# Placing q's high parts from ScalarE's queue in a sliding-window attention kernel

## What is computed

```python
x = L0_attn_hidden_states
xn = _layernorm(x, axis=-1)
# attention
q = _interleaved_rope(q, cos, sin) * SCALE
k = _interleaved_rope(k, cos, sin) * SCALE
scores = jnp.einsum('bquh,bkuh->buqk', q, k)
sw_mask = jnp.abs(pos[:, None] - pos[None, :]) <= SW
scores = jnp.where(sw_mask[None, None, :, :], scores, NEG)
combined = jnp.concatenate([scores, sink_logits], axis=-1)
probs = jax.nn.softmax(combined.astype(jnp.float32), axis=-1)
out = jnp.einsum('buqk,bkuh->bquh', attn, v)
s = jnp.einsum('bquh,uhm->bqm', out, Wo) + bo
# gate
g = _silu(_L0_ffn_ref(xn, L0_ffn_weight, L0_ffn_weight_scale, L0_ffn_bias))
x = x + s * g
```

## Time and profile before

| | us |
|---|---|
| median of three runs | 2087.06 |
| lowest and highest of them | 2068.41, 2089.49 |
| the profiled execution, device time | 2074.46 |
| its span, first to last instruction | 2072.7 |
| TensorE busy, of the span | 1807.7 (87%) |
| VectorE busy | 1277.2 (62%) |
| GpSimd busy | 1011.2 (49%) |
| ScalarE busy | 730.8 (35%) |
| mean granted TensorE clock | 0.907 of full speed |

### The profile page before, as it was taken

One profiled execution on the slowest core, in us unless ns is written; L12 is line 12 of the kernel. 1 busy time (PEld: TensorE's weight loads), 2 busy tenths in 40 slices (PEclk: granted clock), 3 DMA queues, 4 the chain that ended last, 5 costly groups with the idle time before them and its releaser, 6 DMA issues.

```text
span 2072.7 us, 34158 instructions
## 1 busy us (share of the span) xinstructions
PE 1807.7 (87%) x11139; PEld 1592.2 (77%) x11139; DVE 1277.2 (62%) x4157; ACT 730.8 (35%) x1509; POOL 1011.2 (49%) x1019
## 2 busy tenths in 40 slices
PE   2498999989899889898889989898999988899888
PEld 1287878877788777787778878887788877788777
DVE  7755665655656557556566665665666666565564
ACT  2133333333333433333333333343343333333332
POOL 3345444554444644545544553554455465445441
PEclk8579899989998899889999999998999999999899
DMA  4634334344254343443344343344335434442530
GB/s 145 129 68 69 65 63 83 72 78 74 37 94 70 67 78 51 81 75 67 68 78 80 57 88 65 59 92 84 60 53 95 80 64 71 77 66 54 95 65 17
DMA packets 81728, 151.95 MB, mean 73 GB/s; under 512 B 13712, under 2 KB 30864, under 8 KB 77456
## 3 DMA queue, kind: packets, MB, share of 16 engines
q1 hardware_dynamic: 81552, 149.76, 39.8%
HBM read 18.64 MB, written 4.19 MB: 11 GB/s over the span
## 4 chain that ended last, share of the span: by engine, by line
PE 68%; issue 6%; DVE 6%; SPq 5%; ACT 4%; DMA 4%; POOL 3%; POOLq 0%; DVEq 0%
PE pv_bank L1132 23%; PE ring L1093 10%; PE acc L1155 8%; PE ring L1044 8%; PE score L1116 7%; PE score L1118 6%; PE ring L1142 3%; SPq L364 3%; ACT stage L619 2%; PE ring L1053 2%; DMA qT_full<-q_second_hi 2%; DMA kT_low<-k_second 2%; POOL k_first L520 1%; POOL k_second L522 1%; SPq L366 1%
## 5 line engine op out<-in xcount | busy, mean ns | idle before, releaser
L854 DVE CUSTOM_DVE_ANT_0 junk<-ring,mask 128x384 bf16<-128x384 f32 (+1 forms) x1024 | 497.3, 488 | 646.1 <-PE ring L1093 636.2
L1132 PEld LDWEIGHTS pv_bank<-v,stage 128*128 128x128 f32 x5120 | 708.3, 206 | 14.4 <-issue 5.8
L1132 PE MATMUL pv_bank<-v,stage 128*128 128x65 f32 x5120 | 713.8, 282 | 0.6 <-DVE o_norm L886 0.4
L542 POOL TENSOR_SCALAR_AFFINE_SELECT stage<-stage 128x512 f32<-128x512 f32 x384 | 246.8, 656 | 833.9 <-ACT stage L619 833.7
L1093 PE MATMUL ring<-kT_high,qT_full 128*128 128x384 f32 (+1 forms) x1024 | 411.6, 403 | 165.9 <-DMA kT_low<-k_second 71.0
L619 ACT ACTIVATE stage<-score 128x512 f32<-128x512 f32 x640 | 357.5, 597 | 335.5 <-PE score L1118 334.0
L1093 PEld LDWEIGHTS ring<-kT_high,qT_full 128*128 128x128 f32 x1024 | 213.2, 208 | 209.0 <-issue 129.7
L1116 PE MATMUL score<-qT_full,kT_high 128*128 128x512 f32 x640 | 279.0, 436 | 16.1 <-ACT stage L619 14.1
L660 ACT ACTIVATE oT_hi<-ring 128x256 fp32r<-128x256 f32 x256 | 98.6, 385 | 518.5 <-PE ring L1142 518.5
L1118 PE MATMUL score<-qT_high,kT_low 72*128 72x512 f32 x640 | 267.8, 418 | 0.0
L1116 PEld LDWEIGHTS score<-qT_full,kT_high 128*128 128x128 f32 x640 | 132.2, 207 | 68.9 <-ACT stage L619 48.7
(11 more groups left out here) (119 smaller groups left out, 2651.9 us busy)
## 6 DMA issues: line engine op xcount, KB each, us to landing
qT_high<-qT_full SPq DMA_DIRECT2D x64, 512.0 KB, 4.5
qT_full<-q_first SPq DMA_DIRECT2D x64, 256.0 KB, 4.2
qT_full<-q_first_hi SPq DMA_DIRECT2D x64, 256.0 KB, 5.6
qT_full<-q_second SPq DMA_DIRECT2D x64, 256.0 KB, 6.9
qT_full<-q_second_hi SPq DMA_DIRECT2D x64, 256.0 KB, 8.0
kT_high<-k_first_hi SPq DMA_DIRECT2D x128, 64.0 KB, 3.3
kT_high<-k_second_hi SPq DMA_DIRECT2D x128, 64.0 KB, 3.1
qT_high<-turned_rows SPq DMA_DIRECT2D x512, 2.0 KB
```

Source lines behind the costliest of these rows:

```text
L542: nc.gpsimd.affine_select(out=pr, in_=pr, compare_op=ALU.is_ge, fill=0.0, base=0, pattern=[[0, GROUP], [sign, P]], channel_multiplier=-sign) \
L854: nc.vector.tensor_tensor_reduce(junk[:, h % 2, 0:cols], ring[h % 2][:, 0:cols], mask[:, m0:m0 + cols], 1.0, LOWEST, ALU.add, ALU.max, row ...
L1132: last = nc.tensor.matmul(pv[:, h, :], prob[:, q % 2 * 3 + n, h * P:(h + 1) * P], v[:, slot, k, :], start=(n == 0), stop=(n == len(BLOCKS[ ...
```

## The change

SyncE's `queries_in` becomes `lows_in`, which issues only the two transfers of low parts. ScalarE gets `highs_placed(a)`, which issues the two transfers of high parts on its own queue, with the same waits on the scores and on the earlier transfers, and with `s_first_hi` and `s_second_hi` (its own roundings) where SyncE waited for the low parts. It stands in quarter 3 of ScalarE's program, behind `o_high` and ahead of `keys_high`. Sizes, tiles, semaphores and counts of transfers are the same.

```diff
-            def queries_in(a):
+            def lows_in(a):
-                parts = ((0, q_first, q_first_hi, s_first_lo, s_qT_first_in),
-                         (HALF, q_second, q_second_hi, s_second_lo, s_qT_second_in))
                 upto(sp, s_score_pe, NB * (a - 1))
-                for row, low, high, ready, done in parts:
+                for row, low, ready, done in ((0, q_first, s_first_lo, s_qT_first_in),
+                                              (HALF, q_second, s_second_lo, s_qT_second_in)):
                     sp.wait_ge(ready, a + 1)
                     upto(sp, done, Q_IN * a)
                     sp.dma_start(qT_full[row:row + HALF, a % 2, :, :].bitcast(F32), low[:, :]).then_inc(done, 16)
-                    sp.dma_start(qT_full[D + row:D + row + HALF, a % 2, :, :].bitcast(F32), high[:, :]) \
-                        .then_inc(done, 16)
...
+            def highs_placed(a):
+                upto(act, s_score_pe, NB * (a - 1))
+                for row, high, ready, done in ((D, q_first_hi, s_first_hi, s_qT_first_in),
+                                               (D + HALF, q_second_hi, s_second_hi, s_qT_second_in)):
+                    act.wait_ge(ready, a + 1)
+                    upto(act, done, Q_IN * a)
+                    nc.scalar.dma_start(qT_full[row:row + HALF, a % 2, :, :].bitcast(F32), high[:, :]) \
+                        .then_inc(done, 16)
...
                     if q == 1 and real(a):
                         first_high(a)
                         second_high(a)
+                    if q == 3 and real(a):
+                        highs_placed(a)
                     if q == 3 and k in (2, 6) and quad < BATCH * QUADS:
                         keys_high(quad)
```

More of the change, by code:

```diff
@@ L415, in step @@
                 if real(a):
-                    queries_in(a)
+                    lows_in(a)
                 if real(t) and t % QUAD == 0:
```

## The result

The changed kernel takes 2124.69 us (median; 2120.65 to 2142.23), the kernel before 2087.28 us beside it. The ratio is 1.0217, 95% interval 1.0147 to 1.0288: slower by about 45 us, 31 to 60. On a second chip, beside 25 executions of the kernel before, it was 1.0254 (1.0173 to 1.0334). The profiled execution has a span of 2120.1 us against 2072.7, 47.4 more, at a mean clock of 0.908 against 0.907.

The account below looks back on a forecast made before the run. It took TensorE to be bound by its stalls, chiefly waiting for q's landing and the keys, and by its clock. Terms summing to 64.8 us were added to the profiled 2074.46, giving 2139, rounded to 2140; range 2080 to 2190.

Parts of the forecast that it names:

- q's landing is what the first row product waits for: TensorE's unnamed wait is the landing of q's last high part; SyncE's two fewer issues, 1.3 us a step, gain 0.
- k = 3 and 4: 16 boundaries: highs queue behind the lows on the DMA engines, the four need the same 9.96 us, change 0.
- k = 5, 7, 0 and 1: Highs issued behind `o_high` land later at these boundaries, delaying the first row product: 9.6, 6.3, 2.1 and 2.4 us.
- ScalarE held for 1.3 us by two issues: At k = 2 and 6 `keys_high` queues behind the issues, moving 15 boundaries by 1.3 us: 19.5 us.
- ScalarE's next instruction starts at once behind the issues: Sign in the profile after, on ScalarE's queue, that would show the forecast wrong; no size given.
- The rival that the issue is free: Issuing on ScalarE costs nothing and the clock holds; only landings count, 20.4 us, 2095 us; chance 0.24.
- `x_in` ahead of the highs: At k = 7 the load of `x_in` is issued before the highs and competes with them: 1 us, six boundaries, 6 us.
- The clock, 18.9 us: New stalls at k = 5 and 7 drop half of TensorE's full-clock steps there to the low clock: 18.9 us.
- The rival of two queues that add up: Two DMA queues carry more than one, so q's highs land sooner and stalls go: about 2009 us; chance 0.07.
- stalls of 1.1: Sign in the profile after: the first row product at k = 7 and 0 stalls 1.1 us each.

Follow-up runs that it names:

- the repeat: The changed kernel timed once more, unaltered, beside the kernel before on the second chip: 2135.34 us, ratio 1.0254.

## Why the prediction was right, and where its terms were off

It said 2140 us, slower, with 64.8 us added; measured were 37.4 us between the medians, about 45 by the ratio, and 51 between the means on the second chip. Direction and the main mechanism hold; the sum was too large, and that the time came within 16 us of the forecast is in part luck: the sum was added to the fast profiled execution, and on the median of the three runs it would have given 2152. Term by term (the 61 boundaries read here lack one of the eight that it counted at k = 5, and have one more at k = 0 and at k = 1):

- *q's landing is what the first row product waits for; nothing is gained from SyncE's lighter queue.* Right. It is shown by the highs issued with the lows: two issues less on SyncE, and a first row product at 10.06 instead of 10.01. The window that it cites for busy DMA engines (1132 to 1138) lies behind a step with k = 0, not k = 3; behind the one with k = 3 (1223 to 1229) it is the same, share 1.07 and 133 GB/s.
- *k = 3 and 4: no change, since the highs queue behind the lows' bytes.* Right, 10.01 and 10.02.
- *k = 5, 7, 0 and 1: landings 1.2, 0.9, 0.3 and 1.2 us late, 20.4 us.* The mechanism is right, the size about three times too large: the late start on one queue added 6.8 us of stalls at these k. Two inputs of the one formula failed. The issue was put 0.06 us behind the *end* of `o_high`, 0.45 behind its start; it leaves 0.08 behind its start, 0.37 sooner. And the first row product comes 5.96 us behind the first issue, not 6.12 (k = 5: 1310.11 - 1304.15). Together 0.53 off each of the four numbers: for k = 5 that gives 0.68, and it moved by 0.69; for k = 0 it gives less than nothing. With one queue and the same late start, k = 7 moved by 0.2 and k = 0 not at all.
- *ScalarE held for 1.3 us by two issues, 19.5 us at k = 2 and 6.* Held for 1.07, since the first issue overlaps `o_high`; stalls grew by 18.8. That the number fits is part luck: 15 times 1.07 is 16, and the rest arises further down the chain, where at k = 6 GpSimd's subtraction ends 1.5 us later (8.25 against 6.76 behind q's first issue, medians) though the rounding starts 1.07 later. Why is open. Swapping the order of the two showed it as the cause: 19 us of stalls gone at k = 2 and 6 with the issues behind the roundings. The prediction gave "ScalarE's next instruction starts at once behind the issues" as a sign of being wrong. It does start 0.04 us behind the second one's end (1210.88), but that is what an instruction held back by both looks like; the sign was ill chosen. The rival that the issue is free is refuted, but only for an issue that stands ahead of work: behind it, it is free.
- *`x_in` ahead of the highs, 1 us in six boundaries.* About 1.25, shown by putting it back behind them, and the same load behind step 0 (3.0 us), which the sum left out. Like it, the output's store at k = 0 now passes the highs; that was left out of the sum. The 0.3 us at k = 0 that the sum put down to the late start are absent with a late start on one queue, so that store is the likely cause, argued and not tested.
- *The clock, 18.9 us.* A mean clock below 0.907 was to be seen in the profile; it was 0.908, and in the repeat 0.903. Over all executions on the second chip the changed kernel's clock is lower, 0.899 against 0.9105, worth 13 us by that chip's line. So the term was of the right sign and too large. At k = 7 it worked as the prediction had it: half of the steps (4 of 7, in both profiles) started at the low clock, none before. But the stall there was 1.74 us and not 1.1. At k = 5, with a stall of 0.5 and not 1.2, none did; the mean clock of the steps behind k = 5 is lower than before (0.91 against 0.95), but it is 0.91 to 0.93 in the other five profiles without a stall there too, so it is not the stall's doing. The first profile of the changed kernel made up for k = 7 behind k = 3 (0.99 against 0.91), where the stalls are unchanged: chance, as far as these runs show.
- *The rival of two queues that add up* is refuted by the 132 GB/s with both at work. Of the Trainium skill's two statements, the one of "DMA: Bandwidth & Descriptors" ("Issuing engines are not separate DMA queues"), that only the issuing time is saved, the runs bear out: issuing took 1.6 us instead of 2.6 and the landing did not move. The 6% of the page "SBUF — State Buffer" for two transfers at once did not appear: 10.06 against 10.01 us is no gain.

What was expected to be seen at k = 7 and 0 (stalls of 1.1) was 1.74 and 1.09: the second agrees, the first came by another mix than the sum had it, 0.25 of late start and 1.25 of `x_in`, so that the term for `x_in` was too small and that for the late start too large.

## What to carry to other kernels

Where the DMA engines are busy without a gap over a group of transfers, as here, the group ends when its bytes have passed: a second queue gave nothing, and what could be gained lay in an earlier first byte (another buffer slot) and in what stands in front of it. Moving transfers to another queue takes them out of an order that nobody wrote down: whatever stayed on the old queue behind them now runs ahead, so look at every place of the old queue, rare ones like step 0 too. And an issue on a compute engine belongs behind the work that others wait for, where it cost no stall here, not ahead of it.

## What the hardware showed that was not expected

- ScalarE issues a DMA while its previous ACTIVATE still runs, 0.08 to 0.09 us after that one's start, and past ACTIVATEs that it has already taken in. Each issue takes 0.56 us of its queue in the median; the second of a pair took 0.80 where SyncE issued at the same time. An ACTIVATE behind two of them started 1.34 us after the start of the one ahead.
- Transfers of 256 KB from 128 partitions to 32 ran at 132 GB/s with the DMA engines' share at 1.07 to 1.09, on one queue and on two.
- One and the same kernel on one core varied by 3% between executions (2054.19 to 2117.31 us), and the mean granted clock went along, 8.8 to 12.4 us for 0.01 on three chips.
- Behind a stall of 3.6 us or more TensorE's granted clock was low nearly always (164 of 165), behind one of 1.7 to 1.8 us in about half of the cases (107 of 204), and never behind k = 5 and the k = 7 whose median stall is 0.5 us or less (0 of 126).
